# A three-block layer kernel: the softmax-value product, turned round and cut into small products in eight places of the matmul array

## The reference

```python
# first: causal inside each sequence of 64, H = 16 heads of HD = 16
scores = jnp.einsum('bhqd,bhkd->bhqk', q, k) * scale + bias
attn = jax.nn.softmax(scores, axis=-1)
out = jnp.einsum('bhqk,bhkd->bhqd', attn, v)
out = out.transpose(0, 2, 1, 3).reshape(B, S, D)
x = x + jnp.einsum('bsd,ed->bse', out, Wo)
# second: no mask, rotated q and k, then
z = rmsnorm(src + sa @ Wo2)
```

## Time and profile before

| | |
|---|---|
| median of 3 runs | 269.75 us (268.72 to 270.47) |
| the profiled execution, whole | 269.39 us |
| its span in the profile | 267.6 us |
| PE matmul busy | 241.7 us, 90% |
| PE weight loads busy | 215.6 us, 81% |
| DVE busy | 177.3 us, 66% |
| ACT busy | 118.8 us, 44% |
| GpSimd (POOL) busy | 69.5 us, 26% |

### The profile page before, as it was taken

One profiled execution on the slowest core, in us unless ns is written; L12 is line 12 of the kernel. 1 busy time (PEld: TensorE's weight loads), 2 busy tenths in 40 slices (PEclk: granted clock), 3 DMA queues, 4 the chain that ended last, 5 costly groups with the idle time before them and its releaser, 6 DMA issues.

```text
span 267.6 us, 4148 instructions
## 1 busy us (share of the span) xinstructions
PE 241.7 (90%) x1562; PEld 215.6 (81%) x1562; DVE 177.3 (66%) x373; ACT 118.8 (44%) x202; POOL 69.5 (26%) x74
## 2 busy tenths in 40 slices
PE   0988998999989999988977999999889989999991
PEld 0987998998988999967966998787658968998880
DVE  1626783776975998567966686997278556348463
ACT  4423843445176282163814599761363214541000
POOL 4011112032114004111471343797400010340010
PEclk9999999999999999999999999999999999999998
DMA  7999758585616001200001002243000000000010
GB/s 251 341 398 407 227 169 297 191 299 176 170 42 205 2 9 70 81 1 0 4 15 64 2 0 78 82 139 97 0 2 0 0 0 2 0 2 0 21 39 20
DMA packets 8419, 26.11 MB, mean 98 GB/s; under 512 B 1352, under 2 KB 2640, under 8 KB 8144
## 3 DMA queue, kind: packets, MB, share of 16 engines
q1 hardware_dynamic: 8400, 25.86, 28.8%
HBM read 25.33 MB, written 0.52 MB: 97 GB/s over the span
## 4 chain that ended last, share of the span: by engine, by line
PE 76%; DVE 7%; ACT 7%; issue 5%; DMA 2%; POOL 1%; POOLq 0%; SPq 0%; DVEq 0%; ACTq 0%
PE ps L608 70%; PE ps L611 6%; DMA raw<-in_ctx 2%; DVE prob L1108 1%; POOL rstd L394 1%; DVE mx L1107 1%; DVE Z L927 1%; ACT prob L531 1%; DVE on L1120 1%; ACT raw L464 1%; ACT L592 1%; ACT kblk L523 1%; DVE kblk L1162 1%; ACT L579 0%; ACT ks L443 0%
## 5 line engine op out<-in xcount | busy, mean ns | idle before, releaser
L608 PE MATMUL ps<-ch 128*128 128x130 f32 (+1 forms) x208 | 53.4, 273 | 7.2 <-ACT ch L495 7.2
L608 PE MATMUL ps<-ch,cl 128*128 128x260 f32 (+1 forms) x208 | 53.2, 318 | 0.0
L608 PEld LDWEIGHTS ps<-ch 128*128 128x128 f32 (+1 forms) x208 | 41.4, 199 | 7.6 <-ACT ch L495 7.2
L608 PE MATMUL ps<-w,hT 128*128 128x512 f32 x192 | 47.3, 401 | 0.0
L608 PEld LDWEIGHTS ps<-w,hT 128*128 128x128 f32 x192 | 35.7, 188 | 8.9 <-issue 0.5
L608 PEld LDWEIGHTS ps<-ch,cl 128*128 128x128 f32 (+1 forms) x208 | 41.1, 197 | 0.4 <-issue 0.2
L1022 DVE TENSOR_TENSOR cl<-raw,ch 128x1024 fp32r<-128x1024 f32 (+1 forms) x32 | 31.7, 1022 | 12.8 <-ACT ch L495 12.6
L495 ACT ACTIVATE ch<-raw 128x1024 fp32r<-128x1024 f32 (+1 forms) x32 | 27.2, 892 | 15.2 <-PE ps L608 8.2
L394 POOL TENSOR_TENSOR rstd<-ve,half_exp 128x2 f32<-128x2 f32 (+1 forms) x14 | 9.5, 677 | 78.4 <-DVE ve L899 78.2
L608 PE MATMUL ps<-xHL,dense 128*128 128x256 f32 x192 | 24.3, 284 | 1.5 <-DVE xHL L1171 1.5
L608 PEld LDWEIGHTS ps<-xHL,dense 128*128 128x128 f32 x192 | 23.3, 188 | 2.0 <-DVE xHL L1171 1.8
(11 more groups left out here) (160 smaller groups left out, 420.0 us busy)
## 6 DMA issues: line engine op xcount, KB each, us to landing
raw<-in_ctx SPq DMA_DIRECT2D x24, 512.0 KB, 3.9
raw<-in_w SPq DMA_DIRECT2D x8, 512.0 KB, 3.5
w<-in_w SPq DMA_DIRECT2D x2, 1024.0 KB, 9.2
stage<-in_dense SPq DMA_DIRECT2D x4, 512.0 KB, 6.0
mask<-in_mask SPq DMA_DIRECT2D x1, 800.5 KB, 10.4
rows<-in_rows SPq DMA_DIRECT2D x1, 768.0 KB, 8.5
raw<-in_ctx SPq DMA_DIRECT2D x8, 65.0 KB
X<-in_x SPq DMA_DIRECT2D x1, 512.0 KB, 7.2
```

Source lines behind the costliest of these rows:

```text
L608: return pe.matmul(o, l, r, start=start, stop=stop, skip_group_check=not check)
```

## The change

V is no longer moved through the array but loaded into it. `vz` holds V padded with zeros by head parity (for each pair of heads two blocks of 32 columns, one with the even head in its first 16, one with the odd head in its last 16). A product now has 64 rows (the keys of one sequence), 32 weight columns and 64 moving columns (queries). The rows 0 to 63 or 64 to 127 and the four groups of 32 output partitions make eight places of the array. The result comes out with features on partitions at once, so `turn_o` goes. The softmax sums are made by the same products with a constant of ones, `pick`, in place of V; `sums` goes from DVE. DVE divides: a reciprocal of 256 sums on each of 128 partitions, and one multiplication, straight to `aT`. Each tile has 64 such products, 32 with V and 32 with ones. The constants grow from 718 to 782 columns.

```diff
-                ... ("score", 1), ("cross2_product", 5), ("sums", 0), ("cross2", 5), ("split", 22), ("turn_p", 1), ("sums", 1),
-        ("evac", 6), ("values", 0), ("values", 1), ("cross3", 5), ("turn_o", 0), ("turn_o", 1), ("piece", 1),
+                ... ("score", 1), ("cross2_product", 5), ("cross2", 5), ("split", 22), ("turn_p", 1),
+        ("evac", 6), ("values", 0), ("values", 1), ("cross3", 5), ("piece", 1),
...
+    put("pick", np.broadcast_to((np.arange(4 * HD) // HD) % 3 == 0, (P, 4 * HD)))
...
-            def block_values(bank):
-                for bb in range(2):
-                    q = slice(bb * S, bb * S + S)
-                    last = act.activation(vblk[q, :, :, bb, :].rearrange("p t c d -> p (t c) d"),
-                                          ps[q, bank, :].rearrange("p (c d) -> p c d", d=2 * HD), ACT.Copy)
+            def padded_values(bank):
+                got = ps[:, bank, :].rearrange("p (c h d) -> p c h d", h=2, d=HD)
+                for hl in range(2):
+                    last = act.activation(vz[:, :, :, hl, hl * HD:(hl + 1) * HD].rearrange("p t c d -> p (t c) d"),
+                                          got[:, :, hl, :], ACT.Copy)
...
                 elif step == "values":      # PE
                     pe.wait_ge(sem("v"), 2 * (i // 4) + i // 2 % 2 + 1)
                     pe.wait_ge(sem("probT"), 2 * i + 2)
-                    for c in range(H // 2):
-                        last = mm(ps[:, tile_bank(i), c * 4 * HD:(c + 1) * 4 * HD], probT[:, i % 2, c, :],
-                                  vblk[:, i % 2, c, :, :].rearrange("p b d -> p (b d)"), True, True)
+                    spots = [(r, bb) for r in range(4) for bb in range(2)]
+                    for part in range(2):
+                        for j in range(KC):
+                            at = part * P + j * S
+                            for hl in range(2):
+                                for r, bb in spots:
+                                    keys = slice(bb * S, bb * S + S)
+                                    weights = const("pick")[keys, hl * 2 * HD:(hl + 1) * 2 * HD] if part else vz[keys, i % 2, 4 * j + r, hl, :]
+                                    last = mm(ps[32 * r:32 * r + 32, tile_bank(i) + bb, at:at + S], weights,
+                                              probT[keys, i % 2, 4 * j + r, hl * S:(hl + 1) * S], hl == 0, hl == 1)
                     last.then_inc(sem("pv"), 1)
-                elif step == "turn_o":
-                    ...
-                elif step == "sums":        # DVE
-                    link(dve.tensor_reduce(sm[:, k, :], prob[:, k, :, :].rearrange("p c (b k) -> p (c b) k", b=2), AX.X, ALU.add))
-                    link(dve.reciprocal(rs[:, k, :], sm[:, k, :]))
                 elif step == "values":      # DVE
-                    dve.tensor_tensor(on[k] ..., ps[:, tile_bank(k), :] ..., rs[:, k, :] ..., ALU.mult).then_inc(sem("on"), 1)
-                elif step == "turn_o":
-                    link(dve.tensor_scalar(a, both[:, :, 0, :], parity(0), None, ALU.mult))
-                    dve.scalar_tensor_tensor(out=a, in0=both[:, :, 1, :], scalar=parity(1), in1=a,
-                                             op0=ALU.mult, op1=ALU.add).then_inc(sem("aT"), 1)
+                    got = ps[:, tile_bank(k):tile_bank(k) + 2, 0:2 * P].rearrange("p b (w j q) -> p b w j q", w=2, j=KC)
+                    link(dve.reciprocal(over[k][:, :, :, :], got[:, :, 1, :, :]))
+                    dve.tensor_tensor(aT[k][:, :, :, :].rearrange("p j b q -> p b j q"), got[:, :, 0, :, :], over[k][:, :, :, :],
+                                      ALU.mult).then_inc(sem("aT"), 1)
```

More of the change, by code:

```diff
@@ L44 @@
 for _name, _width in (("ident", P), ("parity", 2), ("heads", P), ("causal", S), ("cos", S), ("sin", S),
-                      ("rot", P), ("side", P), ("tile_of", T), ("iota", E)):
+                      ("rot", P), ("pick", 4 * HD), ("side", P), ("tile_of", T), ("iota", E)):
     CONST[_name] = (_at, _at + _width)
@@ L115, in first_half_steps @@
         ("cross3", 6), ("evac", 7), ("score_product", 2), ("score", 2), ("cross4", 6), ("cross1", 7),
-        ("score_product", 3), ("turn_p", 2), ("score", 3), ("piece", 2), ("cross2_product", 7), ("sums", 2),
-        ("turn_p", 3), ("cross2", 7), ("sums", 3), ("values", 2), ("values", 3), ("turn_o", 2), ("turn_o", 3),
+        ("score_product", 3), ("turn_p", 2), ("score", 3), ("piece", 2), ("cross2_product", 7),
+        ("turn_p", 3), ("cross2", 7), ("values", 2), ("values", 3),
         ("cross3", 7), ("project", 2), ("piece", 3), ("project", 3), ("piece", 4), ("cross4", 7), ("xo_product", 1),
@@ L130, in second_half_steps @@
         ("gate_best", 0), ("hidden", 6), ("score", 4), ("hidden", 7), ("score_product", 5), ("shared_product", 0),
[L131 to L133 removed]
+        ("shared_product", 1), ("turn_p", 4), ("piece", 7), ("experts_product", (0, 0)), ("score", 5),
+        ("piece", 8), ("turn_p", 5), ("shared", 0), ("shared", 1), ("experts", (0, 0)), ("values", 4),
+        ("values", 5), ("piece", 9), ("piece", 10), ("project", 4), ("project", 5),
         ("experts_product", (0, 1)), ("experts_product", (0, 2)), ("piece", 11), ("norm2", 1), ("experts", (0, 1)),
@@ L136, in second_half_steps @@
         ("score_product", 6), ("experts", (0, 3)), ("score", 6), ("score_product", 7), ("experts_product", (1, 0)),
-        ("turn_p", 6), ("score", 7), ("experts_product", (1, 1)), ("sums", 6), ("turn_p", 7), ("sums", 7),
-        ("experts", (1, 0)), ("values", 6), ("values", 7), ("turn_o", 6), ("turn_o", 7), ("project", 6),
+        ("turn_p", 6), ("score", 7), ("experts_product", (1, 1)), ("turn_p", 7),
+        ("experts", (1, 0)), ("values", 6), ("values", 7), ("project", 6),
         ("project", 7), ("experts_product", (1, 2)), ("rms1", 1), ("experts", (1, 1)), ("experts", (1, 2)),
@@ L227, in layer @@
     kblk, _ = place("kblk", [P, KC * BH, 4, S])
-    vblk, _ = place("vblk", [P, TH, H // 2, 2, 2 * HD])
+    vz, _ = place("vz", [P, TH, H // 2, 2, 2 * HD])
     prob, _ = place("prob", [P, TH, H // 2, 2 * S])
-    on = [place(f"on{k}", [P, 2, KC, 4, 2 * HD], at=where["prob"] + k * 4096)[0] for k in range(TH)]
+    over = [place(f"over{k}", [P, 2, KC, S], at=where["prob"] + k * 4096)[0] for k in range(TH)]
     aT = [place(f"aT{k}", [P, KC, 2, S], at=where["prob"] + k * 4096 + 2048)[0] for k in range(TH)]
@@ L527, in _ @@
                         act.wait_ge(sem("pv"), 4 * i)
-                    block_values(CHAIN_B)
+                    padded_values(CHAIN_B)
                 elif step == "score":
```

26 lines of the change are left out of this document (3 added, 23 removed).

## The result

The changed kernel takes 279.08 us (median of 4 runs, 277.75 to 279.71) where the kernel before took 269.24 us beside it (268.34 to 270.47, 4 runs). The ratio is 1.034, with a 95% interval of 1.030 to 1.039: slower. The forecast was 277.3 us, in a range of 269 to 289.

The account below looks back on a forecast made before the run. PE was taken to bound the kernel, DVE counting only where PE waits. 269.39 + 21.6 - 14.1 + 0.0 made 276.9 us, or 277.3 against the median of 269.75; range 269 to 289 us.

Parts of the forecast that it names:

- Values products removed: PE, old values steps at four places: four pairs of steps at 3.52 us each go, 14.1 us saved.
- Values products added: PE, eight new steps of 2.7 us, column groups partly overlapping: 21.6 us; bounds for a step 1.8 and 3.5 us.
- The estimates by proportion: PE, scaled from larger products: 0.055 us for a matmul of 64 columns, 0.028 us for a load of 32.
- The larger code ride on DMA queues that are nearly empty: Constants and instruction code: the added 64 columns and larger code were given no cost in the sum.
- 256 of them would need 1.3 us, so issue need not bound: PE instruction issue in a step: at 5 ns each, 256 instructions take 1.3 us, so issue was no limit.
- Reciprocal of 256 elements: DVE division behind the values step: 1.74 us from the slope between reciprocals of 2 and 16 elements; lower bound 0.42.
- Tails: Stretches behind the values steps at the four places with a pair of tiles, until the next dense or context product: 0.0 us together.
- First place: Tail at the first pair of tiles: `cross4` waits for `mb` behind both divisions, 5.6 against 4.36 us, plus 1.2.
- Second place: Tail at the second pair of tiles, up to `xo_product`: 5.3 against 5.89 us, minus 0.6.
- Third and fourth: Tails at the last two pairs of tiles, one projection beside the division: 3.35 against 3.64 us, minus 0.3 each.
- I am wrong from the start if the clock falls: Sign against the forecast: PE's clock falling in the slices of the small products; no size given.
- The rival of full overlap: Column groups overlap fully, 1.8 us for a step, second division waits for the first: 271.7 us, chance 0.19.

Follow-up runs that it names:

- b2_row_order: Changed kernel with the same small products reordered, four in a row in one group of output columns before the next group; 279.99 us, ratio 1.039 to the kernel before.
- c1_folded_sums: Changed kernel with sums and 16 reciprocals back on DVE, spread by a multiplication, turned by four folded-identity products, a cross product between steps; 274.72 us, ratio 1.018.
- d2_small_twice: Kernel before with 64 small products added ahead of the eight large ones of each values step, their sums overwritten; 286.19 us, ratio 1.066.
- a3_twice: Changed kernel with all 64 products of a values step issued twice, same places and result; 313.84 us, ratio 1.163 to the kernel before.

## Why the prediction held, and where it was wrong

The total came out right by two errors that cancel, each of 10 us, and that is luck.

- **Values products removed**, 14.1 us: 14.3 in the table.
- **Values products added**, 21.6 us predicted, 21.4 measured, but built of other things. The products take 11.5 us, not 21.6: column groups overlap fully, 1.25 to 1.35 us for a step without a pause, even under my lower bound of 1.8. The estimates by proportion were too large as well. The Trainium skill ("TensorE: Matmul & The Clock Gate", section "Part 3: Packing small matmuls — row/col tiling") says that small products in different tiles run concurrently; the trace agrees, at 5 ns for each instruction begun.
- **"The larger code ride on DMA queues that are nearly empty"**, at nothing: this is the step that failed. The queue is empty, as I said, yet a block comes every 3.5 us and is used up in 1.3; this costs 9.9 us of pauses. "256 of them would need 1.3 us, so issue need not bound" was true of the engine and left out where the instructions come from. The Trainium skill, in "Advanced Engine Details and Errata", section "ISA Cache", gives lines of 16 KB for 256 instructions; the 128 loads with their matmuls between two pauses agree with it. By that size alone I could have counted 6.75 blocks more; what one costs no row of the kernel before shows: its 12 packets start 15 to 29 us apart, and no pause follows from them.
- **Reciprocal of 256 elements**, 1.74 us: 1.757 measured. The slope of two sizes held to 1%, and the 2.1 us by a repeat count of 8 did not. Taking it away gave 4.4 us of the 5.3 that I had worked out.
- **Tails**, 0.0 us predicted, +1.6 measured, and -0.7 in `b2_row_order` at full clock (16.6 against 17.3): the working of the tails was sound, and as far as one trace shows, the excess came with the clock. First place +1.2 predicted, +2.5 found: the wait for `mb` is there (1.78 us), and part of the stretch ran at 1.2 GHz. Second place 5.3 predicted, 5.07 found. Third and fourth 3.35 predicted, 3.83 and 3.14 found, the third at the lower clock.
- **"I am wrong from the start if the clock falls."** It did, in two stretches, and by `b2_row_order` some 4 us hang on that. This stood among the risks with no price.
- **The rival of full overlap**, 271.7 us at 0.19, was right in its mechanism and wrong in its time, for want of the pauses: with steps of 1.43 us, 9.9 us of pauses and the measured tails it comes to 278.7.

What stays open: why the clock falls in one execution and not in the next of the same kernel. In the profiles it fell in or after stretches in which PE stood still, at places 1 and 3 of the changed kernel and in `c1_folded_sums`; `d2_small_twice` has pauses of 1.36 us and kept it, and so did `b2_row_order` with pauses of up to 2.89. No run separates the length of a pause from what stands around it. Nor is it shown what sets the start of a packet: it lies from 1.2 us before to 1.3 us after the moment at which PE stops, and no run changed the way in which instructions are fetched. And no version tried beats the kernel before.

## What to carry to other kernels

Count the instructions of a packed form before its columns. Here 256 of them were worth 1.3 us of PE, and a block of 256 came every 3.5 us at best; a burst of 256 for a pair of steps, with large products around it, had no pause, and a burst of 512 had one of 1.9 to 3.7 us. To tell such a pause from a wait for data, look whether a packet of the instruction queue starts a fixed time (here 2.4 us) before PE goes on. An operation put on the engine that serves PE costs what PE waits for it, not its duration: leaving out eight divisions of 1.76 us gave 4.4 us, and one spreading copy of 0.29 us kept PE waiting for 4.1. And when a forecast holds, read its terms one by one: this one was right to 1% with two of them off by 10 us.

## What the runs showed of the hardware

- Products of 64 rows and 32 columns in eight places start 5 ns after one another and overlap across column groups in either order tried: 32 take 0.65 us in one and 0.76 us in the other.
- PE stops in a long run of such products, in the changed kernel after 178 to 234 loads with their matmuls, and in `a3_twice` again after each 128 loads with theirs: a new block of 16 KB every 3.5 us at best, and PE goes on 2.2 to 2.7 us after the start of its packet (27 of 29 pauses).
- Large products that follow small tiles take 0.17 us more for a step (1.93 against 1.76 us for eight), and as much stands as a wait ahead of the first small load. That the change of tile is the reason is not shown apart.
- Beside one of POOL's operations on `dense` a DVE copy within SBUF took 2.12 us instead of 0.29, and DVE's operation on `cl` 3.38 instead of 1.22; the division, which reads PSUM, was not held up (1.76 beside POOL's 2.34). The port or lock behind this no run shows.
- A float32 reciprocal costs 6.2 to 6.3 ns for each further element up to 256 (166 ns for 2, 253 for 16, 1757 for 256).
